# A macaron of MoE, attention and Mamba layers on one core: value products in halves, turns and copies moved, scan weights loaded one head ahead

## The reference

```python
# attention: 32 query heads of 8, 8 key/value heads, 1024 tokens
scores = jnp.einsum('bkgqd,bkld->bkgql', qg, k) * SCALE
attn = jax.nn.softmax(scores, axis=-1)
out = jnp.einsum('bkgql,bkld->bkgqd', attn, v)
# scan: 32 heads of 128; per head a projection of x and gate, a convolution,
# products within chunks, states passed between chunks, a gate, a norm over 4 heads
proj = x @ in_proj_w.T
Y_diag = jnp.einsum('bclhn,bcshn,bhcls,bcshd->bclhd', Cc, Bc, Lmat, Xc)
Y_off = jnp.einsum('bclhn,bchdn,bhcl->bclhd', Cc, states_prev, state_decay)
h32 = y * jax.nn.silu(gate.astype(jnp.float32))
return norm_w * h32 @ out_proj_w.T
```

## Time and profile before

| | us |
|---|---|
| median of 3 runs | 1752.1 (1749.7 to 1753.82) |
| the profiled execution | 1751.33 |
| its span, first to last instruction | 1749.4 |
| attention's slots, first to last value product | 266.5 to 658.6 |
| scan of 32 heads | about 1070 to 1642 |

### The profile page before, as it was taken

How to read it: one execution, slowest core, us unless ns; L and a number is a source line. 1 busy time by engine, 2 the same in 40 slices (tenths; PEclk the granted TensorE clock), 3 DMA queues, 4 the chain that set the end, 5 groups by cost and what they waited for, 6 DMA issues and landing times. The chain is left out here.

```text
span 1749.4 us, 24589 instructions
## 1 busy us (share of the span) xinstructions
PE 1500.1 (86%) x7880; PEld 1040.5 (59%) x7880; DVE 1068.8 (61%) x1948; ACT 871.5 (50%) x1268; POOL 488.5 (28%) x422
## 2 busy tenths in 40 slices
PE   3999379999999985899497987898998999999697
PEld 2566333333333334566386765787887888888586
DVE  4121578888888845121376574687767767777475
ACT  1222226666666672222332666575666666675332
POOL 1344320000000000344200012556455555555200
PEclk7999759999999996899799797899999999999899
DMA  8422210000000006532300111323232222321200
GB/s 298 122 46 42 46 25 1 13 13 12 12 12 12 0 1 224 149 48 43 108 1 10 33 33 52 98 75 91 73 91 85 78 84 78 95 93 43 85 1 25
DMA packets 78525, 107.32 MB, mean 61 GB/s; under 512 B 9600, under 2 KB 57984, under 8 KB 78432
## 3 DMA queue, kind: packets, MB, share of 16 engines
q1 hardware_dynamic: 69056, 91.98, 17.0%
q0 software_dynamic: 9376, 14.16, 4.7%
HBM read 89.99 MB, written 11.93 MB: 58 GB/s over the span
## 5 line engine op out<-in xcount | busy, mean ns | idle before, releaser
L971 ACT ACTIVATE attn_probs<-attn_scoresT 128x1024 f32<-128x1024 f32 x256 | 253.9, 1028 | 114.7 <-PE attn_scoresT L1093 114.6
L860 DVE TENSOR_REDUCE attn_max_chunks<-attn_scores 128x1 f32<-128x512 f32 x327 | 214.5, 685 | 40.0 <-PE attn_scores L1077 22.9
L1506 DVE SCALAR_TENSOR_TENSOR ssm_scan_x<-ssm_scan_proj,ssm_w_conv,ssm_scan_x 128x1023 f32<-128x1023 f32 (+2 forms) x96 | 123.1, 1282 | 83.8 <-ACT ssm_scan_x L1501 78.0
L1077 PE MATMUL attn_scores<-attn_k_picks,attn_qT_pass 64*128 64x512 f32 x327 | 144.5, 483 | 19.0 <-DVE attn_max_chunks L860 10.0
L1093 PE MATMUL attn_scoresT<-attn_qT_pass,attn_k_picks 64*128 64x512 f32 x512 | 147.2, 432 | 2.1 <-ACT attn_probs L971 2.0
L401 DVE TENSOR_TENSOR moe_h<-moe_silu,moe_up 128x512 f32<-128x512 f32 x46 | 31.6, 688 | 189.1 <-PE moe_up L516 189.1
L1105 PE MATMUL attn_o<-attn_probs,attn_v_group 128*32 128x512 f32 x1024 | 137.2, 608 | 0.8 <-ACT attn_probs L971 0.8
L1077 PEld LDWEIGHTS attn_scores<-attn_k_picks,attn_qT_pass 64*128 64x128 f32 x327 | 59.6, 192 | 125.5 <-DVE attn_max_chunks L860 104.1
L62 PE MATMUL ssm_scan_proj<-ssm_xnT_hi,ssm_w_in_hi 128*128 128x512 f32 x256 | 112.3, 439 | 22.9 <-DVE ssm_scan_x L1506 21.0
L860 DVE TENSOR_REDUCE attn_max_chunks<-attn_turn 128x1 f32<-128x512 f32 x161 | 110.3, 685 | 28.1 <-PE attn_scores L1077 16.2
L448 ACT ACTIVATE moe_silu<-moe_gate 128x512 f32<-128x512 f32 x46 | 27.5, 598 | 200.0 <-PE moe_gate L516 200.0
(11 more groups left out here) (338 smaller groups left out, 3370.3 us busy)
## 6 DMA issues: line engine op xcount, KB each, us to landing
ssm_cum_all<-ssm_cums SPq DMA_DIRECT2D x32, 512.0 KB, 3.7
ssm_scan_exp_cum<-ssm_cums SPq DMA_DIRECT2D x32, 512.0 KB, 4.0
moe_w_gate_up<-in_moe_w SPq DMA_DIRECT2D x16, 512.0 KB, 10.8
moe_w_up<-in_moe_w SPq DMA_DIRECT2D x16, 512.0 KB, 11.0
moe_w_down<-in_moe_w SPq DMA_DIRECT2D x16, 512.0 KB, 11.1
ssm_w_in<-in_in_w SPq DMA_DIRECT2D x64, 128.0 KB, 3.7
attn_k_picks<-attn_kT SPq DMA_DIRECT2D x32, 128.0 KB, 2.4
ssm_scan_w_out<-in_out_w SPq DMA_DIRECT2D x8, 512.0 KB, 4.1
```

Source lines behind the costliest of these rows:

```text
L860: return nc.vector.tensor_reduce(rmaxc[:, half, place:place + 1], chunk_bank(g, n), AX_X, ALU.max).then_inc(reduced, 1)
L971: nc.scalar.activation(probs[s % 2][:, 2 * pair:2 * pair + 2, :], st_ps[pair][:], ACT.Exp, scale=SCALE).then_inc(exp_done, 1)
L1077: nc.tensor.matmul(chunk_bank(g, n), qm[b][head_rows(j), t * P:(t + 1) * P], kz[b][head_rows(j), j % 2, c * BANK:(c + 1) * BANK], start=Tr ...
L1506: return nc.vector.scalar_tensor_tensor(out[:, shift:], ps[:, :S - shift], w(k), out[:, shift:], ALU.mult, ALU.add)
```

## The change

Five things change, three of them in attention's order of work.

1. `values` makes its four products for queries 0 to 255 (half A), then calls `between`, then makes those for queries 256 to 511 (half B). `between` is the fourth job of a slot: a chunk, or in six slots the turn; the chunk that it displaces then stands behind half B.
2. Turns stand fourth among a slot's jobs instead of first or third; `q2` turns move one slot earlier (6 and 14).
3. Banks are given out by which is free first, where a chunk holds one for 3 jobs and a turn for 5. Before, every job held one for 3.
4. ScalarE's copies stand behind both exponentials of their slot. VectorE's reciprocal and normalisation are parted and stand one slot later, around the second chunk. `LEAD` is 40 instead of 44.
5. In the scan, SyncE issues the input weights of head n+1 between `load_cum(n)` and `load_grow(n)`. Before, they came behind `load_grow(n)` and, every fourth head, behind `load_out`.

```diff
--- before.py
+++ after.py
@@ -590,7 +590,7 @@
 TURNS = (0, 2, 1, 3)
 FINAL_SLOTS = (11, 12)
 PER_SLOT = CHUNKS // SLOTS
-LEAD = HALF + 3 * PER_SLOT
+LEAD = HALF + 2 * PER_SLOT
 LEAD_SCORES_T = 36
 
 
@@ -687,20 +687,23 @@
 
             jobs = [("chunk", ahead, n) for ahead, n in slot_chunks(s)]
             if s in Q1_SLOTS:
-                jobs.insert(0, ("q1", 1, Q1_SLOTS.index(s)))
-            if s == KT_TILES - 1:
-                jobs.insert(0, ("q2", 0, 1))
-            if s == SLOTS - 1:
-                jobs.insert(0, ("q2", 1, 0))
+                jobs.insert(3, ("q1", 1, Q1_SLOTS.index(s)))
+            if s == KT_TILES - 2:
+                jobs.insert(3, ("q2", 0, 1))
+            if s == SLOTS - 2:
+                jobs.insert(3, ("q2", 1, 0))
             if s == 1:
-                jobs.insert(2, ("o", -1, 1))
+                jobs.insert(3, ("o", -1, 1))
             if s == KT_TILES + 1:
-                jobs.insert(2, ("o", 0, 0))
+                jobs.insert(3, ("o", 0, 0))
             return jobs
 
         table = [job for s in range(SLOTS) for job in slot_jobs(s)]
-        bank_of = {job: k % 3 for k, job in enumerate(table)}
-        bank_of[table[-1]] = 1
+        bank_of, free_from = {}, [0, 1, 2]
+        for k, job in enumerate(table):
+            bank = free_from.index(min(free_from))
+            bank_of[job] = bank
+            free_from[bank] = k + (3 if job[0] == "chunk" else 5)
 
         def chunk_bank(g, n):
 
@@ -859,14 +862,18 @@
                 dve.wait_ge(scores_done, CHUNKS * g + n + 1)
                 return nc.vector.tensor_reduce(rmaxc[:, half, place:place + 1], chunk_bank(g, n), AX_X, ALU.max).then_inc(reduced, 1)
 
+            def o_rows(g, half):
+
+                return o_turn_bank(g, half).rearrange("p (t j r) -> p t j r", t=4, r=STACK)
+
+            def reciprocals(g, half):
+                dve.wait_ge(o_turned, 2 * g + half + 1)
+                nc.vector.reciprocal(recip[:], o_rows(g, half)[:, :, :, HD]).then_inc(o_step, 1)
+
             def normalize(g, half):
-
-                rows = o_turn_bank(g, half).rearrange("p (t j r) -> p t j r", t=4, r=STACK)
-                dve.wait_ge(o_turned, 2 * g + half + 1)
-                nc.vector.reciprocal(recip[:], rows[:, :, :, HD]).then_inc(o_step, 1)
                 dve.wait_ge(o_step, 2 * g + half + 1)
                 out = o_tok[:, 4 * half:4 * half + 4, bass.ds(g * GQ * HD, GQ * HD)].rearrange("p t (j r) -> p t j r", r=HD)
-                nc.vector.tensor_tensor(out, rows[:, :, :, 0:HD], recip[:].unsqueeze(3).broadcast_to([P, 4, GQ, HD]),
+                nc.vector.tensor_tensor(out, o_rows(g, half)[:, :, :, 0:HD], recip[:].unsqueeze(3).broadcast_to([P, 4, GQ, HD]),
                                         ALU.mult).then_inc(o_norm, 1)
 
 
@@ -887,11 +894,12 @@
                 for s in range(SLOTS):
                     todo = [(ahead, n) for ahead, n in slot_chunks(s) if not (last and ahead)]
                     for place, (ahead, n) in enumerate(todo):
-                        if place == 2:
-                            outputs(g, s, first)
+                        if place in (1, 2):
+                            outputs(g, s, first, place == 1)
                         reduce(g + ahead, n)
                     if not todo:
-                        outputs(g, s, first)
+                        outputs(g, s, first, True)
+                        outputs(g, s, first, False)
                     if s == 5:
                         top_scores(g, 1)
                     if s == 13 and not last:
@@ -903,17 +911,19 @@
                             if s == FINAL_SLOTS[p] + 3:
                                 add_projected(p)
 
-            def outputs(g, s, first):
-                if s == 1 and not first:
-                    normalize(g - 1, 1)
-                if s == KT_TILES + 1:
-                    normalize(g, 0)
+            def outputs(g, s, first, opening):
+                step = reciprocals if opening else normalize
+                if s == 2 and not first:
+                    step(g - 1, 1)
+                if s == KT_TILES + 2:
+                    step(g, 0)
 
             for n in range(LEAD):
                 reduce(0, n)
                 if n == LEAD_SCORES_T - 1:
                     top_scores(0, 0)
             groups(dve, body)
+            reciprocals(KV - 1, 1)
             normalize(KV - 1, 1)
             for p in range(2, 4):
                 turned_low(p)
@@ -980,17 +990,17 @@
                 first, last = edge(g)
                 for s in range(SLOTS):
                     exp_pair(g, s, 0)
+                    exp_pair(g, s, 1)
                     if s in Q1_SLOTS and not last:
                         copy_q1(g + 1, 1 - b, Q1_SLOTS.index(s))
-                    if s == KT_TILES - 1:
+                    if s == KT_TILES - 2:
                         copy_q2(g, b, 1)
-                    if s == SLOTS - 1 and not last:
+                    if s == SLOTS - 2 and not last:
                         copy_q2(g + 1, 1 - b, 0)
                     if s == 0 and not first:
                         copy_o(g - 1, 1)
                     if s == KT_TILES:
                         copy_o(g, 0)
-                    exp_pair(g, s, 1)
                     for p in range(2):
                         if last and s == FINAL_SLOTS[p]:
                             turned_high(p)
@@ -1094,16 +1104,20 @@
                                             qe[b][head_rows(j), half * BANK:(half + 1) * BANK], start=True, stop=True)
                 last.then_inc(scoresT_done, 1)
 
-            def values(g, b, s):
+            def values(g, b, s, between=lambda: None):
                 half, kt = divmod(s, KT_TILES)
                 pe.wait_ge(exp_done, 2 * (SLOTS * g + s) + 2)
                 if s == 0:
                     pe.wait_ge(vg_in, g + 1)
                 if kt == 0:
                     pe.wait_ge(o_copied, 2 * g + half)
-                for i, j in enumerate(TURNS):
-                    last = nc.tensor.matmul(o_ps[j * STACK:(j + 1) * STACK, :], vg[b][:, kt, :], probs[s % 2][:, i, :],
-                                            start=(kt == 0), stop=(kt == KT_TILES - 1))
+                for part in range(2):
+                    cols = slice(part * (BANK // 2), (part + 1) * (BANK // 2))
+                    for i, j in enumerate(TURNS):
+                        last = nc.tensor.matmul(o_ps[j * STACK:(j + 1) * STACK, cols], vg[b][:, kt, :], probs[s % 2][:, i, cols],
+                                                start=(kt == 0 and part == 0), stop=(kt == KT_TILES - 1), skip_group_check=True)
+                    if part == 0:
+                        between()
                 last.then_inc(pv_done, 1)
 
             def turn_o(g, half):
@@ -1164,15 +1178,13 @@
                                 turn_o(g + ahead, n)
                         return after
 
-                    turn = todo[0][0] != "chunk"
                     scoresT(g, b, s, 0)
-                    scoresT(g, b, s, 1, jobs(3 if turn else 2))
-                    if s % KT_TILES:
-                        jobs(1)
+                    scoresT(g, b, s, 1, jobs(2))
+                    jobs(1)
                     if s > 0:
-                        values(g, b, s - 1)
+                        values(g, b, s - 1, lambda: jobs(1))
                     elif not first:
-                        values(g - 1, 1 - b, SLOTS - 1)
+                        values(g - 1, 1 - b, SLOTS - 1, lambda: jobs(1))
                     jobs(len(todo))
                     if last:
                         for p in range(2):
@@ -1976,20 +1988,28 @@
                 src = out_w[bass.ds(gw * NORM_HEADS * PD, NORM_HEADS * PD), :].rearrange("(j p) d -> p j d", p=P)
                 sync.dma_start(w_out[:], src).then_inc(w_out_in, 16)
 
-            for n in range(G):
-                if n:
-                    load(n, n % 2)
+            def head(n, j):
+                if after(n, 1):
                     load_cum(n)
+                if not is_at(n, LAST):
+                    load(n + 1, (j + 1) % 2)
                 load_grow(n)
+
+            load(1, 1)
+            load_grow(0)
+            for n in range(1, G):
+                head(n, n)
                 if n == NORM_HEADS - 1:
                     load_out(0)
-            with sync.Fori(1, HM // G) as i:
+            with sync.Fori(1, HM // G - 1) as i:
                 for j in range(G):
-                    load(i * G + j, j % 2)
-                    load_cum(i * G + j)
-                    load_grow(i * G + j)
+                    head(i * G + j, j)
                     if j % NORM_HEADS == 0:
                         load_out(2 * i - 1 + j // NORM_HEADS)
+            for n in range(HM - G, HM):
+                head(n, n % G)
+                if n % NORM_HEADS == 0:
+                    load_out(n // NORM_HEADS - 1)
             load_out(G - 1)
 
         @block.gpsimd
```

## The result

The changed kernel takes 1760.8 us (median of 8 runs, 1750.3 to 1782.2), the kernel before 1753.3 in the same session (8 runs, 1749.3 to 1754.2): ratio 1.0045, 95% interval 1.0024 to 1.0067; the one execution of 1782.2 stands apart from the others and is not in the ratio. It is slower by 0.45%. The forecast was 1737, range 1720 to 1753: both sign and range were wrong.

The account below looks back on a forecast made before the run. TensorE and VectorE were taken to wait for each other in attention, and late input weights to hold up the scan. Attention +5 and scan -19.4 gave -14.5 against 1751.33, 1736.8, stated as 1737 us; range 1720 to 1753.

Parts of the forecast that it names:

- Half a value product, 0.57: Attention's slots: four value matmuls of 256 columns take 0.43 plus 0.14 fixed, 0.57 us; bounds 0.50 and 0.64.
- halves cost more: Attention's slots: a value product's fixed part grows with matmul count, 1755 or 1763 us; chance 0.15, shared with costlier turn waits.
- Intervals behind turns, 4.02, 3.66 and 5.0: Attention's slots with a turn: bank waits give 4.02 us for four, 3.66 after q2 at 6, 5.0 after o at 9.
- A group of 51.6: Attention: ten plain slots of 2.69 and six intervals with turns make 51.6 us against 50.34, +1.3 per group.
- First and last group 0 +- 2: Attention's groups 0 and 7: new waits and the copy waits that go about cancel, 0 with 2 us either way.
- The lead: Ahead of attention's slots: `LEAD` takes out four chunks, where two take 1.57 us, giving -3.1.
- Attention about +5: All of attention: six looped groups +8, first and last 0, `LEAD` -3.1; about +5 us, bounds -13 and +23.
- q2 one slot earlier: Attention's q2 turns: GpSimd's last step for the maxima, 0.47 us after a reduction, stays hidden behind half A and three pairs.
- Scan -19.4: Scan: earlier input weights end TensorE's six waits for `x_of`, -19.4 us; 0.5 to 1.5 of each may stay.
- a sign of being wrong: Scan heads still above 18 us, or a half value product at 0.63 us or more, would make the forecast wrong.
- scan gives back half: Scan: `scale_out` or GpSimd behind it holds TensorE up 1.5 us in each of six heads, 1746 us; chance 0.15.
- Turns get cheap: Attention: with short bank waits a turn costs only 0.15 us beyond a plain slot, -44, about 1686 us; chance 0.05.

Follow-up runs that it names:

- halves alone: Kernel before, loop kept, with each value product in two halves of 256 queries and nothing between: 1758.7 us, ratio 1.0046.
- the loads alone: Kernel before with only the change's order of input weight loads in the scan, attention untouched: 1735.9 us, ratio 0.9911.
- the fastest kernel: Changed kernel with query turns holding their bank for 3 jobs instead of 5 and TensorE's eight groups written out: 1717.9 us, ratio 0.9816.
- the shorter turns: Changed kernel with query turns holding their bank for 3 jobs instead of 5, output turns still 5, loop kept: 1738.7 us, ratio 0.9926.

## Why the prediction was wrong

- **Half a value product, 0.57: right.** Half A to the chunk is 0.56 to 0.57 (417.18 to 417.74), and a plain slot 2.69 as worked out. The rival "halves cost more" fell as to the slot. The 60 cycles of overhead per matmul of the Trainium skill ("TensorEngine Tiling (Array Packing)", Performance Considerations, Instruction Overhead), taken one behind the other, would have added 26 us by the prediction's estimate; neither the plain slots (2.69) nor the halves alone (2.71) show any of it.
- **Intervals behind turns, 4.02, 3.66 and 5.0: right.** Measured 4.02 to 4.04, 3.67 and 4.93. A group of 51.6: right, 51.6. That 0.77 of the 4.93 is a wait for `attn_xn` behind one of 0.55 for a reduction was in the sum, but only as 0.9 us of a slot.
- **First and last group 0 +- 2: right**, +0.4 and +1.4 without the clock. The lead was put at -3.1, and attention's first value came 0.6 earlier. It came between 262.0 and 268.7 us in the kernels run here, so the other 2.5 can't be told from what varies there.
- **Attention about +5: wrong.** From first to last value it was to be +8 (+5 with the lead), and is +30. Of the 22 missing, 21 are TensorE's lower clock and its idle time at the jump, which no term and no rival held. The sum took the clock of the kernel before, 1.00 in all slots, as given. It priced the added waits at their own length, and the added matmuls at their time in the array, and not at what 256 more matmuls (128 products) in the loop's body do where TensorE jumps back.
- **q2 one slot earlier: right**, hidden; no wait for the top scores shows ahead of a q2 turn.
- **Scan -19.4: right as a number, in part by luck.** It was -18.6 in the profiled pair and -17.7 from gated product to gated product with the loads alone. ScalarE's wait went from 34.1 in 7 places to the first:

```profile
ACT ssm_w_in_hi L2204 <- DMA ssm_w_in<-in_in_w: 4.2, 1, 4.2
```

  TensorE's wait for `x_of`, 19.4 in 6 places, is no longer among the waits. The turn of a head follows the products directly, with no idle time ahead of it, where the earlier trace rows had 2.83:

```profile
1280.47 1.83 PE L2329 MATMUL ssm_scan_y<-ssm_scan_c_exp_cum,ssm_scan_states 128*128 128x128 f32 x14
1282.13 1.04 PE L2302 MATMUL ssm_scan_turn<-main_ident,ssm_scan_x 128*128 128x128 f32 x8
```

  The two heads at an output load take 34.5 to 34.9 us where they took 36.3 to 37.9, four times, and 34.0 and 33.6 for 37.9 and 37.1 at the first and the last: 1.8 to 3.9 gained by each of the six pairs, 17.0 in all; the other 1.6 came in the scan's first head. Two heads still took 18.7 and 18.3, which the prediction had named as a sign of being wrong.

  What TensorE had waited for is not simply gained, though. A wait for GpSimd stands where there was next to none, before and after:

```profile
PE ssm_scan_turn L2301 <- POOL ssm_scan_x_to_end L2026: 0.6, 2, 0.3
```
```profile
PE ssm_scan_turn L2321 <- POOL ssm_scan_x_to_end L2046: 8.4, 6, 1.8
```

  It comes once in each of the six pairs, 1.3 to 1.8 us long: GpSimd waits for the output weights before it scales them, and its later steps come late by that much (GpSimd, the head of the 1.28 us wait at 1305.42):

```profile
1297.35 2.28 POOL L2060 TENSOR_TENSOR ssm_scan_w_out<-ssm_scan_w_out,ssm_norm_w 128x1024 f32<-128x1024 f32 x1 [1.70 <-DMA ssm_scan_w_out<-in_out_w]
```

  This gives back 7.8 of the 19.4. What made up for it is the term that the sum lacked in attention too, the clock. Behind four of the six long waits for `x_of` the kernel before fell to half the clock for 3.4 us (at 1214.8, 1354.8, 1423.1 and 1559.6), and three times behind waits of 3.4 us at the scan's start. After the change two such stretches are left of seven, both at the start. From first to last gated product TensorE's idle time fell by 11.0 us (40.7 to 29.8) and its busy time, for the same 2878 matmuls, by 7.6 (480.7 to 473.0).
- **Rival "scan gives back half": its cause came, its time did not.** `scale_out` does hold TensorE up by 1.3 to 1.8 us in each of six heads, where the rival had 1.5; the clock hid it. "Turns get cheap" did not come in this change, but part of it did in the fastest kernel: 12.6 us less than before from first to last value, where the rival had put 44.

The failing step was thus one: the sum for attention, slots of 2.69 us plus intervals behind turns, put the cost of a falling clock and of the jump back at nothing. It holds only while the instructions arrive and the clock stays up; this missed 21 us. With the jumps written out and the banks as predicted, the kernel takes 1743.6, 7 above the forecast of 1737 and inside its range, with two falls of 1.5 us left. The 1717.9 of the fastest kernel is no proof of the forecast, since it needs the shorter turns too, whose intervals the prediction did not work out.

## What to carry to other kernels

A sum of intervals at full clock has a condition: look for the longest time that TensorE stands idle in each slot before and after, since here slots with at most 0.55 us of it never lost the clock and those with 0.77 or more did now and then, at 1.5 to 4.5 us each, most of them soon after an earlier fall. The same holds for a gain: a long wait that goes can give back the clock as well. Count TensorE's instructions in a hardware loop's body too: an edit that is free in the array cost 3 us of idle time and a fall of the clock at each of two jumps back (13 us in all in the changed kernel), and writing the loop out gave it back. A bank that a slower reader empties sets how soon the next job can use it: give each kind of job its own hold, and measure each.

## What the runs showed of the hardware that I had not expected

- TensorE stood idle for 2.7 to 3.6 us at the jump back of its hardware loop, with nothing to wait for that the profile shows, once the body had grown by 256 value matmuls (7880 to 8904 in the whole program). The instruction queue moved 32 packets from 266 to 700 us instead of 10. Written out, the same instructions caused no gap, with 26 packets, so the number of packets alone does not bring it. That TensorE waits there for its own instructions is inferred, not seen.
- The Trainium skill ("TensorE: Matmul & The Clock Gate", "A second HAM failure mode: psum-queue depth-cycling") describes a kernel whose clock went back and forth because TensorE idled briefly and often between groups of matmuls. The runs agree that short idle times can do it: here the clock fell behind waits of 0.77 us, with 0.55 ahead of them. They add that it falls behind some of the equal waits only (the table above), nearly always 30.7 us after a rise; why is open.
- Twice as many value matmuls of half the columns cost the same: 16 in 1.00 us where 8 took 1.00.
